# GpSimd's order in the first attention: an iteration's scatters issued ahead of the rounded context parts and the weight piece

## What is computed

```python
x = x + jnp.tanh(g_xattn[0]) * _L0_xattn_ref(_layernorm(x, axis=-1), ctx_1024, ctx_1024, ...)   # 16 heads of 16
x = x + jnp.tanh(g_ffn[0]) * _L0_ffn_ref(_layernorm(x, axis=-1), ...)
# in _L0_ffn_ref: a second layernorm, logits over 8 experts, top 2 of them, each an MLP 256 -> 1024 -> 256
logits = xf @ Wg.T + bg
tp, ti = jax.lax.top_k(probs, K)
x = x + jnp.tanh(g_xattn[1]) * _L1_xattn_ref(_layernorm(x, axis=-1), ctx_1024, ctx_1024, fside_BxS2_0, ...)
x = x + jnp.tanh(g_ffn[1]) * _L1_ffn_ref(_layernorm(x, axis=-1), ...)                            # 16 slots, soft
```

## Time and profile before

| what | value |
|---|---|
| median of 3 runs | 1365.84 us (1363.78 to 1376.23) |
| the profiled execution's own time | 1366.23 us |
| its span in the trace | 1364.3 us |
| mean granted TensorE clock | 0.979 of full speed |
| PE busy | 1297.8 us, 95% |
| DVE busy | 926.3 us, 68% |
| ACT busy | 794.6 us, 58% |
| POOL busy | 714.0 us, 52% |

### The profile page before, as it was taken

One profiled execution on the slowest core, in us unless ns is written; L12 is line 12 of the kernel. 1 busy time (PEld: TensorE's weight loads), 2 busy tenths in 40 slices (PEclk: granted clock), 3 DMA queues, 4 the chain that ended last, 5 costly groups with the idle time before them and its releaser, 6 DMA issues.

```text
span 1364.3 us, 38216 instructions
## 1 busy us (share of the span) xinstructions
PE 1297.8 (95%) x14806; PEld 1154.1 (85%) x14806; DVE 926.3 (68%) x2484; ACT 794.6 (58%) x1759; POOL 714.0 (52%) x712
## 2 busy tenths in 40 slices
PE   6999999998899999999999988999999999899898
PEld 5888888886899999999999966899999998555476
DVE  5898988886576555565665026999999997312287
ACT  4666666662477777777776334656666565332454
POOL 1456565553367778777776033666666652100131
PEclk9999999997999999999999987999999999999999
DMA  6665454543567776767776811631111110599811
GB/s 197 229 222 183 148 181 149 182 160 98 196 193 226 226 224 216 228 223 221 220 224 221 341 43 33 218 122 55 56 49 48 49 45 13 193 431 430 338 59 67
DMA packets 103618, 237.24 MB, mean 174 GB/s; under 512 B 8976, under 2 KB 85904, under 8 KB 91024
## 3 DMA queue, kind: packets, MB, share of 16 engines
q1 hardware_dynamic: 97296, 218.02, 46.8%
q0 software_dynamic: 6144, 16.79, 3.9%
HBM read 173.96 MB, written 60.82 MB: 172 GB/s over the span
## 4 chain that ended last, share of the span: by engine, by line
PE 82%; DVE 8%; DMA 4%; issue 2%; ACT 2%; SPq 1%; POOL 1%; DVEq 0%; ACTq 0%; PEldq 0%; POOLq 0%
PE ps L1515 12%; PE psT L1500 6%; PE ps L590 5%; PE psS L567 5%; PE ps L782 5%; PE ps L730 4%; PE psT L576 4%; PE psS L1500 3%; PE ps L1500 3%; PE ps L603 3%; PE ps L715 2%; PE ps L744 2%; PE ps L654 2%; PE psT L582 2%; DMA arena<-w_dram 2%
## 5 line engine op out<-in xcount | busy, mean ns | idle before, releaser
L1468 POOL TENSOR_TENSOR wb_lo<-arena,wb_hi 128x2048 fp32r<-128x2048 f32 x64 | 296.4, 4632 | 99.5 <-ACT wb_hi L1588 99.5
L576 PE MATMUL psT<-arena 32*128 32x128 f32 x2048 | 156.1, 289 | 0.0
L1515 PE MATMUL ps<-wb_hi,hT_hi 128*128 128x256 f32 x528 | 153.3, 290 | 2.5 <-DVE hT_lo L1641 2.4
L1515 PE MATMUL ps<-wb_lo,hT_hi 128*128 128x256 f32 x528 | 148.3, 281 | 0.0
L1515 PE MATMUL ps<-wb_hi,hT_lo 128*128 128x256 f32 x528 | 148.3, 281 | 0.0
L567 PE MATMUL psS<-arena 32*128 32x256 f32 x1024 | 144.5, 400 | 1.4 <-ACT arena L940 0.7
L1588 ACT CAST wb_hi<-arena 128x1024 fp32r<-128x1024 f32 x128 | 130.7, 1046 | 13.1 <-DMA arena<-w_dram 12.8
L576 PEld LDWEIGHTS psT<-arena 32*128 32x128 f32 x2048 | 130.1, 190 | 2.2 <-issue 1.1
L1146 POOL TENSOR_TENSOR arena<-arena,eps_sb 128x1 f32<-128x1 f32 x96 | 26.4, 275 | 200.2 <-DVE arena L1020 113.6
L567 PEld LDWEIGHTS psS<-arena 32*128 32x128 f32 x1024 | 94.8, 192 | 14.3 <-issue 11.2
L1653 DVE TENSOR_TENSOR arena<-ps,arena 128x512 f32<-128x512 f32 (+1 forms) x39 | 25.4, 650 | 115.7 <-PE ps L1515 75.3
(11 more groups left out here) (375 smaller groups left out, 3892.9 us busy)
## 6 DMA issues: line engine op xcount, KB each, us to landing
arena<-wset_dram SPq DMA_DIRECT2D x24, 2048.0 KB, 15.6
xs_rows<-arena SPq DMA_DIRECT2D x33, 1024.0 KB, 8.7
arena<-w_dram SPq DMA_DIRECT2D x32, 1028.0 KB, 6.0
arena<-w_dram SPq DMA_DIRECT2D x32, 1024.0 KB, 6.0
arena<-w_dram SPq DMA_DIRECT2D x7, 2052.0 KB, 12.4
w_sb<-xs_rows SPq DMA_DIRECT2D x33, 256.0 KB, 2.8
xs_rows<-arena SPq DMA_DIRECT2D x33, 256.0 KB, 5.7
arena<-ctxT_dram SPq DMA_DIRECT2D x63, 128.0 KB, 2.3
```

Source lines behind the costliest of these rows:

```text
L576: nc.tensor.matmul(psT[:, b, j * P:(j + 1) * P], kbd[p, (k - 1) % 3, c, par, :], qT[p, (k - 1) % 3, c, :], start=j == 0, stop=False, skip_ ...
L1468: nc.gpsimd.tensor_tensor(wb_lo[:, u % 2, part], wb_raw[:, u % 2, part], wb_hi[:, u % 2, part], ALU.subtract).then_inc(w_g.sem, 1)
L1515: last = nc.tensor.matmul(ps[5][:, t * D:(t + 1) * D], hp[:, f, t * P:(t + 1) * P], wp[:, f, :], start=f == 0 and t == 0 and n == 0, stop= ...
```

## The change

In POOL's program of the first attention the block that issues the scatters of block k - 4 is moved up. It now stands behind the bias (L1200) and ahead of the context's parts and the weight piece. Nothing is added or removed, and the programs of PE, DVE, ACT and SP are the same as before, instruction for instruction. With the move the scatters' line number becomes L1219, and the weight piece's L1228; L1163 and L1165 keep theirs.

```diff
-                    if A and valid(k + 2) and k + 2 >= ctx_first:
-                        context_parts(k + 2)
-                    if A and 8 <= k < 24:
-                        o = E0 + (k - 8) * 256
-                        pool.wait_ge(first_hi, k - 7)
-                        last = nc.gpsimd.tensor_tensor(wb_lo[:, 0, o:o + 256], wb_raw[:, 0, o:o + 256],
-                                                       wb_hi[:, 0, o:o + 256], ALU.subtract)
-                        if k == 23:
-                            last.then_inc(ring_ready, 1)
                     if A and valid(k - 4):
                         pool.wait_ge(zeroed[k % 2], dma_at(k - 4, k % 2))
                         if valid(k - 1):
...
                                 out_offset=bass.IndirectOffsetOnAxis(ap=slot_i[:, c, k - 4:k - 3].bitcast(U32), axis=0),
                                 in_=xn[:, (k - 4) % 3, :], in_offset=None).then_inc(scat[k % 2], 16)
+                    if A and valid(k + 2) and k + 2 >= ctx_first:
+                        context_parts(k + 2)
+                    if A and 8 <= k < 24:
+                        o = E0 + (k - 8) * 256
+                        pool.wait_ge(first_hi, k - 7)
+                        last = nc.gpsimd.tensor_tensor(wb_lo[:, 0, o:o + 256], wb_raw[:, 0, o:o + 256],
+                                                       wb_hi[:, 0, o:o + 256], ALU.subtract)
+                        if k == 23:
+                            last.then_inc(ring_ready, 1)
```

## The result

The changed kernel takes 1374.34 us (median of 22 runs), the kernel before beside it 1368.18 us (22 runs): a ratio of 1.0058 with a 95% interval from 1.0040 to 1.0077, that is +7.9 us, between +5.5 and +10.5; the two medians themselves are 6.2 apart. The forecast was +10.2. The profiled execution took 1375.81 us with a span of 1373.9, 9.6 more than the span before.

The account below looks back on a forecast made before the run. A loop between DVE and PE was taken to bound the first attention; +2.0 us (ten iterations) and +8.2 (sixteen, net) made +10.2, so the median goes from 1365.84 to 1376.0 us, range 1362.6 to 1382.

Parts of the forecast that it names:

- The bound and POOL's times: First attention: DVE-PE loop sets the pace; scatters start 1.00 us after the mark (L1067's start), moved parts have room.
- The first meeting: DVE's L977 is held until POOL's ctx_lo (a context part) ends, so L1000 starts 0.2 us later.
- The ten iterations: First-attention iterations without a weight piece: 0.2 us more each, +2.0 us together.
- The second meeting: In iterations with a weight piece, DVE's L982 is held until the piece ends: +0.71 us, making 10.24.
- The sixteen: First-attention iterations with a weight piece, k = 8 to 23: from 9.73 to 10.24 us each, +8.2 us net.
- What those sixteen have to give back: Iterations with a piece take 9.73, not 9.53: late scatters go with late L877; earlier scatters should remove this 0.2 us.
- 1: Rival: ctx_lo and the piece don't hold DVE, and earlier scatters pay: -3.2 us, 1362.6; chance 0.12.
- 2: Rival: L977's 0.2 us is paid, but L982 gets past the piece: +2.0 us, 1367.8; chance 0.17.
- The lower bound of rows 11: Earlier trace: DVE's L1047, two SBUF inputs, took 0.17 us beside POOL's L1148; kept as lower bound for the hold.
- Rival 3: DVE's L1114 loses the gap behind ctx_hi to ctx_lo and ends 0.78 us late: +19, 1384.8; chance 0.15.
- the forecast's own range: With L982 held for 0.6 to 0.85 us, the kernel takes 1373.5 to 1379 us; the forecast's chance is 0.50.

Follow-up runs that it names:

- e0: The kernel before the change, unchanged, profiled again: 152.83 us from k = 8 to 24, where the first trace has 155.66.
- e1: Changed kernel with the weight piece moved behind L1187, the context's parts still behind the scatters: 1362.59 us against 1360.26 for the kernel before, ratio 1.0017.
- e4: Changed kernel with DVE's L982 written as a reduction of one SBUF operand in place of an addition of two: ratio 1.0033 to the kernel before.
- e8: The changed kernel, unchanged, profiled and timed again: 1375.9 us against 1366.26 for the kernel before, ratio 1.007.
- e5: Kernel before with the weight piece behind L1187 and the first scatter also waiting for PE's next step, starting at 1.47: 152.84 us from k = 8 to 24.
- e10: Repeat of e5, unchanged, to try late scatters on another chip: 152.75 us from k = 8 to 24.
- e2: Against the kernel before, only the weight piece goes behind the scatters, the context's parts staying ahead of them: ratio 1.0029.
- e6: Kernel before with the weight piece behind L1187 and a POOL memset of 128x1024 added behind the scatters: iterations of 9.95 us.
- e9: The changed kernel, unchanged, a third profiled execution: 259.56 us from k = 4 to 30.

## Why the prediction was right, and where its sizes were off

**The bound and POOL's times.** Right. The scatters start 1.00 us after the mark from k = 5 to 29, the parts and the piece run behind them at 3.43, 3.94 and 4.63 after the mark, and L590 waits for nothing.

**The first meeting.** The mechanism was right, and the size 0.2 measured 0.15 in most iterations. L977 ends where the forecast put it, but L1000 had 0.1 us of slack of its own. In e0 iteration 26, PE and DVE:

```profile
273.14 0.38 PE L567 MATMUL psS<-arena 32*128 32x256 f32 x2
```

```profile
273.35 0.22 DVE L988 SCALAR_TENSOR_TENSOR arena<-const,arena 128x2 f32<-128x2 f32 x1
273.57 1.22 DVE L1000 TENSOR_REDUCE arena<-psS 128x8 f32<-128x1024 f32 x1
```

L1000 reads the scores that PE finishes at 273.52, and starts then, 0.22 after L988's start. In the changed kernel it starts 0.13 after L988's. So the first tenth of a microsecond of any delay is free. The ten iterations cost 0.97 (k = 4 to 7) and 0.72 (k = 24 to 29), +1.7 in place of +2.0. They are not alike: k = 4 costs 0.40, since L1099 is held there too, k = 5 costs 0.24, and k = 29 nothing.

**The second meeting.** L982 ends 5.38 us after the mark in place of 4.66, +0.72 where 0.71 was forecast; L1000 again moved about 0.1 less. So 10.16 and not 10.24. The sixteen cost +6.9 in place of +8.2, and the stage +8.6 in place of +10.2. e1 and e4 show this step by taking the meeting away: 9.69 and 9.81 in place of 10.16.

**What those sixteen have to give back.** The L877 of before was late in two of its three traces, and on time, with the same scatters, in the third. The stage of before thus takes 251.0, 252.0 or 248.2 us from k = 4 to 30, the changed one 259.6 in all three traces: +8.6 and +7.6 against the first two, and +11.4 against the third, though no trace of the changed kernel is from a chip where L877 was on time. The timed +7.9 and, in e8's runs, +9.6 lie among these. That the late scatters "go together with" a late L877 was read from one trace and used as a cause. On both chips of the first group where late scatters ran it is wrong (e0 and e5 on one, e10 on the other). Elsewhere the cause isn't shown: there L877 is late in before's sixteen only, the changed kernel's are at 4.06 to 4.12, and the piece's old place is as good an explanation as the scatters. So this term of 3.2 us came true against the trace that it was read from, for a reason that nothing shows; against e0 there was nothing to give back. That part of the hit is luck. What makes L877 late stays open. The trace names PE's L782, which had ended by 3.90 in either case.

**The rivals.** 1 and 2 fall with L977 and L982. The lower bound of rows 11 stands beside them and isn't refuted: L1047, with two SBUF inputs, kept 0.17 to 0.18 us under L1148 in the changed kernel too, in all 26 iterations. What sets L1148 apart from ctx_lo and the piece no run here tests. Rival 3 falls: L1114 keeps 0.41 us from k = 5 on; but its mechanism exists, since in e2, where the piece stands directly behind the scatter, and in iteration 4 of the changed kernel, L1099 and L1114 are held (L1099 0.40 and 0.57), and in e6 both are. The chances have a slip: the forecast's own range ends at 1379, and yet 0.09 of its chance is put above 1379.5.

**The rest of the span.** Outside of the stage, the first trace has +1.0. That is a small sum of larger things: +0.3 up to the mark of k = 4, +0.7 from that of k = 30 to PE's L1515 in the first experts, +3.1 from there to the second attention, -1.8 in it and -1.3 behind it. The +3.1 holds the same mechanism, in the expert stage. There POOL's L1468 runs for 4.6 us at a time, and DVE's short planning chain L1318 to L1342 falls across it. The changed kernel, POOL, DVE and PE:

```profile
392.45 4.62 POOL L1468 TENSOR_TENSOR wb_lo<-arena,wb_hi 128x2048 fp32r<-128x2048 f32 x1 [0.56 <-ACT wb_hi L1588]
398.25 4.52 POOL L1468 TENSOR_TENSOR wb_lo<-arena,wb_hi 128x2048 fp32r<-128x2048 f32 x1 [1.18 <-ACT wb_hi L1588]
```

```profile
392.49 4.60 DVE L1325 TENSOR_TENSOR arena<-arena 128x8 f32<-128x8 f32 x1
...
398.59 4.20 DVE L1341 TENSOR_SCALAR unit_s<-arena 1x6 int32<-1x6 f32 x1
```

```profile
404.92 0.55 PE L1515 MATMUL ps<-wb_hi,hT_hi 128*128 128x256 f32 x1 [5.55 <-DVE hT_lo L1641]
```

Two instructions of 8 and 6 elements per partition stand for 4.6 and 4.2 us, and PE stands for 5.55 (1.98 before). In e9, the same kernel, L1341 falls between two of POOL's instructions:

```profile
406.98 0.22 DVE L1341 TENSOR_SCALAR unit_s<-arena 1x6 int32<-1x6 f32 x1
```

and PE waits 0.8. The first hit (L1325 or L1327, in some kernels with numbers 2 higher) is in all fourteen traces, the second (L1341 or L1342, with PE waiting 5.5 to 5.8 us) in six: two of the changed kernel's three, none of before's three, four of the other eight. So it is a draw that the change may load but doesn't decide. Where the first hit falls on L1327 (five traces), the second never comes.

The stretches outside of the stage vary by themselves as well, and the granted clock there with them. e6 has a stage of 258.50, 10.3 longer than e0's, and a span only 1.2 longer, though neither has the second hit. Up to the mark of k = 4 e0 is 2.7 longer, with a granted clock of 0.67 from 20 to 30 us where e6 has 1.00 (e9 has 0.66 there, and is 3.7 longer up to that mark than e8 at 1.00); from the mark of k = 30 to L1515 e0 is 4.5 longer, at 0.76 against 0.83; and behind the second attention 2.5 longer. From 60 to 300 us all fourteen traces have 1.00. With both the second hit and these stretches a single span says little about a change of 5 us, and the marks of the stage say much more.

## What to carry to other kernels

Before moving work on GpSimd, list what VectorE runs at the new time, and look there for casts, tensor_scalars and operations with two SBUF inputs: each can be held to the end of GpSimd's instruction, however small it is, while reductions kept their time in the traces here. Not every GpSimd instruction holds: L1148, on one column, never held L1047. A term that is read from one trace as two things that go together needs a second trace of the same kernel before it enters a sum; and a gain of a few microseconds is better read from the marks of its stage than from the span.

## What the runs showed that I had not expected

- Tiny instructions can be the dearest: a cast of 1x6 elements took 4.50 us in e2 (L1342) for 0.15 of its own, and L1325 or L1327, of 8 columns, took 4.5 to 4.6 us in every trace, for 0.16 to 0.17 us of their own.
- A memset by GpSimd holds a VectorE cast and a tensor_scalar as an instruction that reads does (1.24 and 0.89 us in e6, for 0.21 and 0.40).
- The scatters themselves hold DVE, over a part of their 1.06 us. With the scatter at 1.00 the cast L1075 takes 0.36 us in place of 0.17, when it starts 0.67 us into it; with the scatter at 1.5, as in iteration 12 before, L1075 keeps 0.18 and it is L1089 that takes 0.61 in place of 0.41. So the move exchanged one hold of 0.2 us for another, which the prediction had not counted.
- The same kernel's first attention from k = 4 to 30 is 248.2 or 251 to 252 us long, by the execution or the chip, through one ACT instruction, L877, at 3.95 or 4.4 to 4.6 us after the mark.
